# Second scan of a two-layer block: the state product of a chunk cut into two products of 64 rows, and its product, decay and addition moved to the head of a step

## What is computed

```python
Y_diag = jnp.einsum('bcthn,bcshn,bhcts,bcshp->bcthp', Ch, Bh, Lmat, x)
decay_states = jnp.exp(dA_cum[..., -1:] - dA_cum)
states = jnp.einsum('bcshn,bhcs,bcshp->bchpn', Bh, decay_states, x)
chunk_decay = jnp.exp(_segsum(jnp.pad(dA_cum[..., -1], ((0, 0), (0, 0), (1, 0)))))
states = jnp.concatenate([jnp.zeros_like(states[:, :1]), states], axis=1)
prev = jnp.einsum('bhzc,bchpn->bzhpn', chunk_decay, states)[:, :-1]
Y_off = jnp.einsum('bcthn,bchpn,bhct->bcthp', Ch, prev, jnp.exp(dA_cum))
return (Y_diag + Y_off).reshape(b, l, h, p)
```

## Time and profile before

| | before |
|---|---|
| median of 3 runs | 1266.36 us (1265.95 to 1267.1) |
| profiled execution, its time | 1271.14 us |
| its span | 1269.4 us |
| TensorE busy in the span | 1032.2 us, 81% |
| VectorE busy | 916.2 us, 72% |
| ScalarE busy | 489.1 us, 39% |
| GpSimd busy | 466.8 us, 37% |
| chain that ended last | TensorE 33% of the span, VectorE 11%, DMA 5%, ScalarE 4% |

### The profile page before, as it was taken

How to read it: one execution, slowest core, us unless ns; L and a number is a source line. 1 busy time by engine, 2 the same in 40 slices (tenths; PEclk the granted TensorE clock), 3 DMA queues, 4 the chain that set the end, 5 groups by cost and what they waited for, 6 DMA issues and landing times.

```text
span 1269.4 us, 18530 instructions
## 1 busy us (share of the span) xinstructions
PE 1032.2 (81%) x6024; PEld 600.7 (47%) x6024; DVE 916.2 (72%) x1506; ACT 489.1 (39%) x1114; POOL 466.8 (37%) x333
## 2 busy tenths in 40 slices
PE   3987997888887878773587778989889988888895
PEld 2354455444444444442434444555545555455453
DVE  4767768899888889897486655766768666755576
ACT  2200235455544445451130144544554444434442
POOL 0000103788888788762270003222313222123310
PEclk9988999898988889995888889989999999899897
DMA  7950443878878787899620134433433333234413
GB/s 228 366 128 0 126 79 105 148 129 148 147 139 159 127 155 134 147 148 213 134 63 1 26 79 97 97 81 81 100 89 81 90 81 79 64 81 106 95 28 133
DMA packets 111188, 143.25 MB, mean 113 GB/s; under 512 B 30023, under 2 KB 97335, under 8 KB 110903
## 3 DMA queue, kind: packets, MB, share of 16 engines
q0 software_dynamic: 34464, 77.92, 33.5%
q1 hardware_dynamic: 76630, 64.14, 18.1%
HBM read 72.80 MB, written 39.46 MB: 88 GB/s over the span
## 4 chain that ended last, share of the span: by engine, by line
PE 33%; DVE 11%; DMA 5%; ACT 4%; issue 3%; POOL 1%; SPq 1%; ACTq 0%; DVEq 0%; POOLq 0%
PE bank L1846 5%; PE bank L1434 4%; PE bank L1427 4%; PE bank L1890 3%; DMA sum<-yo,to_i 3%; DVE cv L2091 2%; PE bank L698 2%; PE bank L1829 2%; PE bank L1912 2%; PE bank L1876 2%; PE bank L1838 2%; PE bank L1870 1%; PE bank L686 1%; DMA x<-sum 1%; DVE areaD L2036 1%
## 5 line engine op out<-in xcount | busy, mean ns | idle before, releaser
L1500 POOL DMA_INDIRECT sum<-yo,to_i x48 | 76.9, 1602 | 361.4 <-ACT yo L1454 359.1
L1164 POOL DMA_INDIRECT sum<-yo,to_i x80 | 156.0, 1950 | 47.5 <-issue 39.9
L1171 POOL DMA_INDIRECT xg<-xn_d,token_i x80 | 103.1, 1289 | 174.7 <-DVE to_i L460 92.2
L1011 PE MATMUL bank<-areaA,xgT 128*128 x320 | 133.0, 545 | 15.2 <-issue 8.8
L1028 PE MATMUL bank<-areaA,hidT 88*128 x320 | 96.7, 427 | 41.5 <-ACT hidT L1076 29.8
L2036 DVE TENSOR_TENSOR areaD<-areaD,gb 128x512 f32<-128x512 f32 x128 | 87.5, 689 | 41.9 <-ACT areaD L1983 32.8
L1144 DVE TENSOR_TENSOR_SCAN xnT<-areaB,xnT 128x1024 f32<-128x1024 f32 x42 | 96.3, 2292 | 3.3
L1028 PEld LDWEIGHTS bank<-areaA,hidT 88*128 88x128 f32 x320 | 57.7, 201 | 76.5 <-issue 71.4
L1983 ACT ACTIVATE areaD<-bank 128x512 f32<-128x512 f32 x128 | 76.1, 594 | 44.7 <-PE bank L1838 42.6
L1011 PEld LDWEIGHTS bank<-areaA,xgT 128*128 128x128 f32 x320 | 62.9, 215 | 61.6 <-issue 46.6
L686 PE MATMUL bank<-xnT,areaB 128*128 128x512 f32 x192 | 86.8, 599 | 0.8 <-DVE y L716 0.8
(11 more groups left out here) (338 smaller groups left out, 2201.9 us busy)
## 6 DMA issues: line engine op xcount, KB each, us to landing
y<-xnT POOLq DMA_DIRECT2D x21, 1024.0 KB
wst<-gu_f SPq DMA_DIRECT2D x96, 176.0 KB
y<-areaB POOLq DMA_DIRECT2D x11, 1024.0 KB
wst<-down_f SPq DMA_DIRECT2D x48, 176.0 KB
areaA<-in_gu SPq DMA_DIRECT2D x2, 2816.0 KB
gu_f<-in_gu POOLq DMA_DIRECT2D x1, 5632.0 KB, 16.8
sum<-yo SPq DMA_DIRECT2D x2, 2176.0 KB, 16.2
down_f<-in_down POOLq DMA_DIRECT2D x1, 2816.0 KB, 22.5
```

Source lines behind the costliest of these rows:

```text
L1011: last = nc.tensor.matmul(bank[:, GB + q % 2, 0:2 * FI], xgT[:, q % 2, k, :], wgu0_of(e, k), start=(k == 0), stop=(k == KD - 1))
L1164: nc.gpsimd.indirect_dma_start(sum0_d[q % 2], bass.IndirectOffsetOnAxis(ap=to_i[:, q:q + 1], axis=0), yo[:, q % 5, :], None, compute_op=AL ...
L1171: nc.gpsimd.indirect_dma_start(xg[:, q % 5, :], None, xn_d[0], bass.IndirectOffsetOnAxis(ap=token_i[:, q:q + 1], axis=0)).then_inc(s.gathe ...
L1500: nc.gpsimd.indirect_dma_start(sum1_d, bass.IndirectOffsetOnAxis(ap=to_i[:, q:q + 1], axis=0), yo[:, q % 4, :], None, compute_op=ALU.add). ...
```

## The change

The state product is cut by its rows. Each half multiplies 64 rows (one half of the heads) by 256 columns, so `xd` needs no zeros and has half the columns. One half goes into the bank ST, the other into a ring bank as a new piece `st`, that VectorE frees. The ring banks are now 1 and 3 and ST is 2, so that the two halves always stand in neighbouring banks and one instruction of VectorE adds both. CS moves to bank 0. S and the reading of CS now have the heads ordered by half. The pair of products stands ahead of `gb` on TensorE. The decay and the addition stand between `ys` / `gated` / `gate_silu` and the writing of `xq` and `xd` on VectorE. One memset (L1510) of GpSimd falls away.

```diff
-        xd = sb("xd", [P, 2, HP, 2, HD], F32, c1)
+        xd = sb("xd", [P, 2, HP, HD], F32, c1)
...
-        ST, XT, CS, YB, EB = 2, 5, 3, 4, 6
+        RINGS = (1, 3)
+        ST, XT, CS, YB, EB = 2, 5, 0, 4, 6
...
             if n < CHUNKS:
+                if step:
+                    PIECES.append((b, "st", step))
                 PIECES.append((b, "gb", step))
...
-            return bank[:, k, :], ring_full[k]
+            return bank[:, RINGS[k], :], ring_full[k]
...
-            poo.done(nc.gpsimd.memset(xd[:, :, :, :, :], 0.0))
...
+                if n < CHUNKS and step:
+                    taken(pe, b, "gb", old)
+                    pe.wait_ge(xt_used, n)
+                    o, full = make(pe, b, "st", step)
+                    in_ring = AT[b, "st", step] % 2
+                    for hf in (1 - in_ring, in_ring):
+                        r = slice(hf * Q, (hf + 1) * Q)
+                        nc.tensor.matmul((o if hf == in_ring else bank[:, ST, :])[:, 0:HP * HD], gb[r, old % 2, Q:Q + P], xd[r, old % 2, :, :].rearrange("p n d -> p (n d)"),
+                                         start=True, stop=True).then_inc(full if hf == in_ring else st_full, 1)
                 if n < CHUNKS:
                     if step == 0:
                         pe.wait_ge(conv_out, b * 6 + 6)
...
-                if n < CHUNKS and step:
-                    taken(pe, b, "gb", old)
-                    pe.wait_ge(xt_used, n)
-                    nc.tensor.matmul(bank[:, ST, :], gb[:, old % 2, Q:Q + P], xd[:, old % 2, :, :, :].rearrange("p n h d -> p (n h d)"),
-                                     start=True, stop=True).then_inc(st_full, 1)
...
+                if n < CHUNKS and step > 1:
+                    if step == 2:
+                        v.wait_ge(dec_in[b % 2], 16 * (b // 2 + 1))
+                    v.wait_ge(yo_full, b * (CH - 1) + old)
+                    state_of(v, b, old)
+                    s4 = S[:, :].rearrange("p (h n d) -> p h n d", h=2, d=HD)
+                    decayed = vec.done(nc.vector.tensor_tensor(s4, s4, dec[:, b % 2, old, :].rearrange("p (n h) -> p h n", h=2).unsqueeze(3)
+                                                               .to_broadcast([P, 2, HP, HD]), ALU.mult))
+                if n < CHUNKS and step:
+                    take(v, b, "st", step)
+                    v.wait_ge(st_full, b * (CH - 1) + step)
+                    k = AT[b, "st", step] % 2
+                    added = bank[:, RINGS[0] + k:RINGS[0] + k + 2, 0:HP * HD]
+                    s2 = S[:, :].rearrange("p (h c) -> p h c", h=2)
+                    if step > 1:
+                        v.wait_ge(vec.sem, decayed)
+                        nc.vector.tensor_tensor(s2, s2, added, ALU.add).then_inc(s_ready, 1)
+                    else:
+                        if b:
+                            v.wait_ge(yo_full, b * (CH - 1))
+                        nc.vector.tensor_copy(s2, added).then_inc(s_ready, 1)
+                    state_of(v, b, step)
+                    v.sem_inc(ring_free[k], 1)
                 if n < CHUNKS:
                     v.wait_ge(xt_full, n + 1)
...
-                    if g == 1 and n < CHUNKS and step > 1:
...
-                        decayed = vec.done(nc.vector.tensor_tensor(s3, s3, dec[:, b % 2, old, :].unsqueeze(2).to_broadcast([P, HEADS, HD]), ALU.mult))
-                    if g == 2 and n < CHUNKS and step:
-                        v.wait_ge(st_full, b * (CH - 1) + old + 1)
-                        if step > 1:
-                            v.wait_ge(vec.sem, decayed)
-                            nc.vector.tensor_tensor(S[:, :], S[:, :], bank[:, ST, :], ALU.add).then_inc(s_ready, 1)
```

More of the change, by code:

```diff
@@ L1259, in _program @@
         xq = sb("xq", [P, 2, HP // 2, 3, 2, HD], F32, c1)
-        xd = sb("xd", [P, 2, HP, 2, HD], F32, c1)
-        w_dt_raw = xd[:, :, :, :, :].rearrange("p a n h d -> p (a n h d)")[:, 0:KD * 6 * HP].rearrange("p (k n) -> p k n", k=KD)
+        xd = sb("xd", [P, 2, HP, HD], F32, c1)
+        w_dt_raw = xd[:, :, :, :].rearrange("p a n d -> p (a n d)")[:, 0:KD * 6 * HP].rearrange("p (k n) -> p k n", k=KD)
         wst = sb("wst", [P, WR, WF], F32, c1)
@@ L1368, in take @@
             eng.wait_ge(ring_full[k], n + 1)
-            return bank[:, k, :], ring_free[k]
+            return bank[:, RINGS[k], :], ring_free[k]
         def taken(eng, *name):
@@ L2118, in scan1_vector @@
                     v.wait_ge(yo_full, ob_ * (CH - 1) + old)
-                    nc.vector.tensor_tensor(ys[half, :].rearrange("p (h d) -> p h d", d=HD), bank[half, CS, :].rearrange("p (h d) -> p h d", d=HD),
-                                            ecn[half, t, ob_, :, :].rearrange("p n h -> p (n h)").unsqueeze(2).to_broadcast([half.stop - half.start, HEADS, HD]),
+                    nc.vector.tensor_tensor(ys[half, :].rearrange("p (n h d) -> p h n d", h=2, d=HD), bank[half, CS, :].rearrange("p (h n d) -> p h n d", h=2, d=HD),
+                                            ecn[half, t, ob_, :, :].rearrange("p n h -> p h n").unsqueeze(3).to_broadcast([half.stop - half.start, 2, HP, HD]),
                                             ALU.mult).then_inc(y_tok, 1)
@@ L2132, in scan1_vector @@
                             x_half = bank[r, XT, 0:HP * HD].rearrange("p (a u d) -> p a u d", u=2, d=HD)
-                            to = (xq[r, step % 2, :, 0:3:2, hf, :], xd[r, step % 2, :, hf, :].rearrange("p (a u) d -> p a u d", u=2))[z]
+                            to = (xq[r, step % 2, :, 0:3:2, hf, :], xd[r, step % 2, :, :].rearrange("p (a u) d -> p a u d", u=2))[z]
                             last = nc.vector.tensor_tensor(to, x_half, dw[r, z, step, b, :].rearrange("p (a u) -> p a u", u=2).unsqueeze(3)
@@ L2136, in scan1_vector @@
                     last.then_inc(xt_used, 1)
+                if n < CHUNKS:
                     taken(v, b, "gb", step)
```

## The result

| | before | changed |
|---|---|---|
| median | 1266.15 us (1264.86 to 1267.1, 4 runs) | 1282.47 us (1276.01 to 1288.01, 4 runs) |
| ratio, 95% interval | | 1.0124 (1.0088 to 1.0160) |
| profiled execution | 1271.14 us | 1282.40 us |

The change makes the kernel 1.2% slower. The forecast was 1263.4 us, with a range up to 1272. Run again on another chip beside the experiments it gave 1.0132 (1.0101 to 1.0163). The kernel before had medians from 1259.7 to 1268.2 us on the other chips, and its single executions on one chip lay up to 1% from the median, so what follows compares ratios to the kernel before on the same chip, and rows of single profiles. The ratios leave out executions over 1.5% above the fastest of the same kernel, which are 4 of the 12 of ys_even and 1 of the 29 of the kernel before beside it.

The account below looks back on a forecast made before the run. The prediction took TensorE to bound the kernel, busy 421 of 472 us in the second scan. Its terms, -4.3 + 2.3 + 2.5 + 2.5 + 2.5 - 5.4 - 2.4 - 0.7 = -3.0, took 1266.4 to 1263.4 us; range 1256 to 1272.

Parts of the forecast that it names:

- TensorE, removed and added: At each head on TensorE, the state product's 0.97 us gives way to a pair of products costing 0.64, 0.33 less.
- the rival of halves in turn: The two half products on TensorE do not run side by side: slower, 1270 us; chance 0.14.
- 13 heads win 0.33: Four first steps of a sequence and 9 odd heads each win 0.33 us on TensorE: -4.3 us.
- An ordinary even head loses 0.1: Group 0 waits for VectorE's addition; 9 even heads lose 0.1 to 0.5 us, mostly 0.1: +2.3 us.
- The state is early: L1912's three waits for the state go, -5.4 us; the clock may stay up, -2.4; at step 14's end, -0.7.
- Step 4 follows the stall below: Remark leaving step 4 out of the even heads' loss, because it follows the stall at the end of step 3.
- The late heads, +2.5 and +2.5: Steps 11 and 19 lose 0.3 us each and step 3 1.95, together +2.5; step 28 another +2.5.
- The clock, -2.4: Without L1912's waits the clock may stay up; of 2.7 us lost behind step 3 and 0.9 in step 31, -2.4.
- The sign of being wrong: Wrong if L1876's successor costs over 0.97, group 0's addition waits exceed 10 us, or L1427's idle time outgrows its gain.
- The later start of `xq`, +2.5: VectorE starts `xq` 0.64 to 0.86 us late; idle time absorbs it except in steps 2, 10, 18, 28 to 31: +2.5.
- It goes back into other waits: Rival: a quarter of the 12.8 us gained is waited for at the experts, giving 1266.6 us; no separate chance given.
- VectorE's head gates the step: Rival: group 0's ring bank and `xq` behind two state operations make it slower, 1270 us; chance 0.17.

Follow-up runs that it names:

- ys_even: The changed kernel with `ys` of even steps moved behind the addition, `gated` left ahead of it; 1276.68 us, ratio 1.0109 to the kernel before.
- pe_move_only: The kernel before with only the whole state product moved ahead of `gb`, decay and addition left in groups 1 and 2; 1273.80 us, ratio 1.0021.
- whole_head: The kernel before with the whole state product ahead of `gb`, decay and addition at VectorE's head, no ring piece; 1266.69 us, ratio 0.9986.
- whole_wait: whole_head with one wait added: TensorE waits at group 0 until the addition is done; 1278.41 us, ratio 1.0136 to the kernel before.
- product_first: The changed kernel with TensorE's first products of the chunk before put ahead of group 0's segment sum; 1265.98 us, ratio 1.0049 to the kernel before.
- ys_behind: The changed kernel with decay and addition put ahead of `ys` and `gated`; 1289.20 us, ratio 1.0149 to the kernel before.

## Why the prediction was wrong

By its own steps:

- *TensorE, removed and added: 0.97 for 0.64.* Right: 0.63 in all 28. Records of the two row halves pair, the rival of halves in turn falls. A window that ends 0.09 after the first start holds two records already:

```profile
926.33 0.49 PE L1867 MATMUL bank<-xd,gb 64*128 64x256 f32 x2
```

- *13 heads win 0.33.* Right for the heads that VectorE does not hold, such as step 15. (Step 1 waits 0.09.)
- *An ordinary even head loses 0.1.* Mis-sized: 0.33 in step 10. I chose 0.03 between decay and addition and 0.12 for the hand-over; it is 927.99 - 927.85 = 0.14, where the code has three semaphore waits ahead of the addition, and 928.88 - 928.68 = 0.20.
- *The state is early: the three waits of L1912 go, -5.4, and the clock may stay up, -2.4.* **This is the step that failed.** The waits went, but I gave their time to the sum without asking what TensorE meets next. "Step 4 follows the stall below" set that head at nothing; it waited 3.37 there. The old wait of step 3 and the new one of step 4 are one lag, VectorE's, and the change added `ys`, decay and addition to it before TensorE is let go. Steps 3 and 4 together, before:

```profile
819.26:853.79 34.53, 30.83 (x251) 17.49 (x250) 25.46 (x50) 14.82 (x35) 8.06 (x7) 0.90 0.37 85
```

and changed:

```profile
816.64:855.35 38.71, 32.28 (x255) 18.22 (x255) 25.75 (x50) 15.08 (x35) 8.06 (x7) 0.87 0.34 76
```

They take 4.2 us more, where the terms for them (+1.95, -2.86 and most of the -2.4) come to about -3.
- *The late heads, +2.5 and +2.5.* Steps 3 and 28 right (2.32 and 2.77 waited, 2.3 and 2.8 worked out); step 20, which was counted as an ordinary one, waited 1.55, step 30 1.08. All heads together were to lose 3.0 (-4.3 + 2.3 + 2.5 + 2.5). Measured, 28 pairs won 9.2 and some 17 were waited: they lost 8.
- *The clock, -2.4.* This term had the wrong sign. Measured 58 us at half clock in the scan in place of 38. If TensorE is busy in those 20 us as it is on the whole (87%), that is 20 x 0.87 x 0.5 = 9 us, an estimate; the two clocks are read to 0.01, which leaves it open by some 3 us. So the profiled scan adds up as -9 for the pair, +14 of idle time and +9 of clock: +14 for the 13.6 seen. Between the forecast of -3.0 and this lie 16.6 us, of which the heads make 5 and the clock 11.
- *The sign of being wrong.* "Over 10 us of waits for the addition at group 0" came, with 16.6. But the terms of the forecast have 11.6 us of such waits themselves (7.3 lost in the late and even heads, and the 0.33 won in each of those 13), so the limit was set below the forecast.
- *The later start of `xq`, +2.5.* Not contradicted: pe_move_only and whole_head bound it to at most 0.5%, some 6 us, together with what they win.
- *The rivals.* "It goes back into other waits" is not what came: TensorE's idle time ahead of the experts' second product fell from 22.1 (L1427) to 21.3 us (L1430), that ahead of the transposes of `hid` grew from 12.8 (L1421) to 15.3 (L1424). "VectorE's head gates the step" had 0.17 and 1270. It named the right place, group 0's ring bank, but priced the other half of itself, the late `xq`. I weighed it by the mean idle time of VectorE, while two thirds of the waiting is in five heads in which VectorE is behind.

That VectorE's lag, carried over the ring bank, is the cause is shown by whole_wait and whole_head: the wait alone brings the loss, and without it the same order of VectorE costs nothing. What share the clock has is an estimate between 7 and 9 us of 16 or 17; no run changed the clock alone.

## What to carry to other kernels

Before a buffer is shared, ask who frees it and what stands ahead of the freeing on that engine, and look at the few steps in which that engine is late: here five of 28 heads had two thirds of the waiting. A wait that disappears is a gain only after the next meeting of the same two engines has been worked out. Where a wait cannot be avoided, work can be moved into it (product_first won 10 us, though not surely by this alone), and moving the freeing instruction forward must not push back another one that someone waits for (ys_behind).

## What was not expected

- Two f32 products on 64 rows each, with 256 columns, take 0.63 us with the change of shape, for 0.97 of one with 128 rows and 512 columns. Their records run as first and first (0.01 apart), then second and second (0.32 later).
- A wait of some 2 to 3 us can cost its step more than itself. Step 28 takes 19.95 us in whole_wait (wait 2.37) and 15.01 in whole_head (none); step 4 takes 21.56 (wait 2.19) and 18.63 (0.41). Other steps gave some of it back (steps 15 to 17, above). In the changed kernel the window view around step 4 shows the clock behind such a wait:

```profile
832.00:836.00 4.00, 2.32 (x25) 1.37 (x24) 3.93 (x8) 1.98 (x5) 0.88 (x1) 1.00 0.47 83
836.00:840.00 4.00, 2.31 (x19) 1.21 (x20) 3.65 (x9) 0.73 (x2) 0.00 (x0) 0.71 0.00 0
```

- The kernel before itself spreads by 1250.68 to 1272.28 us over 29 runs on one chip, with mean clocks from 0.912 to 0.931. The fastest has 0.929, the slowest 0.918 and not the lowest, so the clock goes with a part of the spread only. Differences of 0.2% need more runs than the first three suggested.
